# A gated delta rule layer: 8x8 diagonal blocks by substitution on GpSimd instead of three doubling levels, a new order of pieces, and a reordered first stage

## What is computed

```python
h = rmsnorm(x, rms1_w)
q = short_conv(h @ Wq, conv_q_w).reshape(b, t, H, DK)      # 4 taps, then silu; k and v likewise
q, k = (l2norm(q), l2norm(k))
g = -jnp.exp(A_log) * jax.nn.softplus(h @ Wa + dt_bias)
beta = jax.nn.sigmoid(h @ Wb)
def step(S, inp):                                          # scanned over the 256 tokens
    qt, kt, vt, gt, bt = inp
    S = S * jnp.exp(gt)[..., None, None]
    mem = jnp.einsum('bhk,bhkv->bhv', kt, S)
    delta = (vt - mem) * bt[..., None]
    S = S + jnp.einsum('bhk,bhv->bhkv', kt, delta)
    return S, jnp.einsum('bhk,bhkv->bhv', qt * scale, S)
o = rmsnorm(o, gnorm_w) * jax.nn.silu(h @ Wg)
out = x + o.reshape(b, t, VD) @ Wo                         # then the layer's feed-forward part
```

## Time and profile before

| | |
|---|---|
| median of 3 runs | 2594.49 us |
| the profiled execution, its own time | 2592.89 us |
| its span, from the first to the last instruction | 2590.9 us |
| PE busy | 2481.9 us (96%) |
| PE weight loads | 2064.9 us (80%) |
| DVE busy | 2049.2 us (79%) |
| ACT busy | 1700.1 us (66%) |
| POOL busy | 905.7 us (35%) |

### The profile page before, as it was taken

The page is one execution under the profiler, slowest core; times in us unless marked ns, Lnnn a source line. Parts: engine busy times, 40 slices in busy tenths (PEclk is TensorE's granted clock), DMA queues, the critical chain, the costliest instruction groups (busy, mean ns, idle before and its releaser), DMA issues. The chain is left out here.

```text
span 2590.9 us, 59545 instructions
## 1 busy us (share of the span) xinstructions
PE 2481.9 (96%) x22000; PEld 2064.9 (80%) x22000; DVE 2049.2 (79%) x4279; ACT 1700.1 (66%) x3907; POOL 905.7 (35%) x1065
## 2 busy tenths in 40 slices
...
DMA packets 147551, 118.36 MB, mean 46 GB/s; under 512 B 24306, under 2 KB 128699, under 8 KB 147267
## 3 DMA queue, kind: packets, MB, share of 16 engines
...
## 5 line engine op out<-in xcount | busy, mean ns | idle before, releaser
L808 DVE TENSOR_TENSOR dr_w<-dr_ps,mask 128x512 bf16<-128x512 f32 x768 | 526.2, 685 | 88.3 <-PE dr_ps L624 87.8
L822 DVE SCALAR_TENSOR_TENSOR dr_y<-dr_ps,cw,dr_y 128x255 f32<-128x255 f32 (+2 forms) x1152 | 475.7, 473 | 27.1 <-ACT dr_y L938 27.1
L924 ACT CAST dr_tn<-dr_ps 128x512 bf16<-128x512 f32 x640 | 375.2, 586 | 156.0 <-PE dr_ps L637 155.3
L927 ACT CAST dr_tt<-dr_ps 128x512 bf16<-128x512 f32 x768 | 458.7, 597 | 20.7 <-PE dr_ps L644 20.7
L721 PE MATMUL dr_ps<-dr_w,dr_am 128*128 128x96 f32 x3072 | 417.7, 279 | 9.7 <-ACT dr_w L984 2.1
L721 PEld LDWEIGHTS dr_ps<-dr_w,dr_am 128*128 128x128 f32 x3072 | 378.4, 192 | 32.4 <-ACT dr_w L984 24.7
L938 ACT ACTIVATE dr_y<-dr_ps,cw 128x256 f32<-128x256 f32 x384 | 161.3, 471 | 209.9 <-PE dr_ps L661 209.7
L644 PE MATMUL dr_ps<-dr_tt,dr_w 128*128 128x128 bf16 x3072 | 297.3, 219 | 0.9 <-DVE dr_w L808 0.9
L624 PE MATMUL dr_ps<-dr_tn,dr_b 128*128 128x128 bf16 x3072 | 297.1, 219 | 0.0
L1050 POOL TENSOR_SCALAR_AFFINE_SELECT dr_b<-dr_b 128x512 bf16<-128x512 bf16 x128 | 81.9, 640 | 503.7 <-ACT dr_b L974 503.7
L637 PEld LDWEIGHTS dr_ps<-dr_w,dr_tt 128*128 128x128 bf16 x2560 | 186.5, 101 | 84.1 <-issue 49.0
...
## 6 DMA issues: line engine op xcount, KB each, us to landing
...
dr_qk<-dr_sy SPq DMA_DIRECT2D x384, 48.0 KB, 2.0
...
dr_bcb<-scr_b SPq DMA_DIRECT2D x128, 64.0 KB, 4.8
dr_qk<-dr_sy SPq DMA_DIRECT2D x128, 32.0 KB, 1.9
...
```

The costliest lines, as they stand in the source:

```text
L808: v.tensor_tensor((tn if l == 0 else w16)[:, us, :], ps[:, (X0, X1)[g], :].rearrange("p (u n) -> p u n", u=QH), bc(mask[:, l, :], 1, QH), ...
L822: v.scalar_tensor_tensor(y[:, slot, x:T], ps[:, BANK[n], off:off + T - x], cw[:, t, TAPS - 1 - x:TAPS - x], y[:, slot, x:T], ALU.mult, ALU ...
L924: act.copy(tn[:, us, :], ps[:, (X2, X1)[g], :].rearrange("p (u n) -> p u n", u=QH)).then_inc(s["tn_ok"], 1)
L927: act.copy(dst, ps[:, (X0, X2)[g], :].rearrange("p (u n) -> p u n", u=QH)).then_inc(s["tt_ok"], 1)
```

## The change

- `LEVELS` is 4, starting with blocks of size 8 (`LVL0` = 3). The 8x8 diagonal blocks are inverted first: 8 DMAs (`blocks`) copy the diagonal blocks out of `b16` into `c16`; piece `rows` spreads their rows over the partitions with 14 matmuls of 64 columns against selection matrices `sel`, and ACT copies the result to `ab`; piece `base` on GpSimd does the substitution, a copy and 14 small tensor operations, each behind a wait for the one before; piece `expand` on DVE places the 8x8 inverses into 128x128 matrices `tn` and `tt` (a product with a mask, a 32x32 transpose, two products of 128x1024 elements).
- GpSimd's part of `gains` is cut: the root and the scaled keys become pieces `root` and `keys_gain` with places of their own.
- `PLAN` is new; its last piece stands at 56.42, the levels lie between 30.2 and 37.79, the gates come last among an iteration's first pieces, in two PSUM banks.
- `hb` is gone: the projections and gates read `hT`. The gates' weights are loaded on a semaphore of their own.
- In `prepare`: the gate signs are computed on GpSimd, which also makes `sel`; `spread` is issued ahead of `steps`; `scr_b` is written from ACT's queue; the reciprocal and the transposes of `beta` move into `delta_rule`'s first iteration.

```diff
+BASE = 8
-LEVELS = 7
+LEVELS = 4
+LVL0 = 3
-PLAN = ((0.44, ("proj", 0)), (1.01, ("taps", 0, 0)), (2.07, ("proj", 1)), (2.47, ("taps", 0, 1)),
...
+PLAN = ((0.56, ("proj", 0)), (1.72, ("taps", 0, 0)), (2.25, ("taps", 0, 1)), (2.98, ("proj", 1)),
+        (3.59, ("silu", 0)), (3.92, ("taps", 1, 0)), (4.27, ("proj", 2)), (4.33, ("taps", 1, 1)),
+        (4.97, ("taps", 2, 0)), (6.86, ("silu", 1)), (7.7, ("taps", 2, 1)), (7.98, ("gains",)), (8.07, ("norms",)),
+        (8.18, ("keys",)), (8.73, ("silu", 2)), (9.39, ("decays", 0)), (9.46, ("scores", 0)),
+        (9.96, ("decayed", 0, 0)), (10.89, ("decayed", 0, 1)), (11.01, ("decays", 1)), (11.38, ("scores", 1)),
+        (11.92, ("decayed", 1, 0)), (12.74, ("negate", 0)), (12.95, ("decayed", 1, 1)), (13.84, ("negate", 1)),
+        (14.35, ("gate", 0)), (14.42, ("gate", 1)), (15.57, ("root",)), (15.61, ("keys_scale",)),
+        (17.44, ("keys_gain",)), (19.4, ("values", 0)), (21.73, ("values", 1)), (23.28, ("rows",)),
+        (26.88, ("base",)), (29.49, ("expand",)), (30.2, ("merge1", 0, 0)), (30.59, ("merge2", 0, 0)),
+        (30.85, ("merge1", 0, 1)), (32.0, ("merge2", 0, 1)), (32.2, ("merge1", 1, 0)), (33.32, ("merge2", 1, 0)),
+        (33.82, ("merge1", 1, 1)), (34.02, ("merge2", 1, 1)), (34.12, ("merge1", 2, 0)), (34.66, ("merge2", 2, 0)),
+        (34.95, ("merge1", 2, 1)), (35.48, ("merge2", 2, 1)), (36.24, ("merge1", 3, 0)), (36.95, ("merge2", 3, 0)),
+        (37.4, ("round", 0)), (37.53, ("merge1", 3, 1)), (37.79, ("merge2", 3, 1)), (37.94, ("w0", 0)),
+        (38.12, ("residual", 0, 0)), (38.32, ("delta", 0, 0)), (40.47, ("residual", 0, 1)), (40.93, ("delta", 0, 1)),
+        (42.47, ("state_out",)), (43.86, ("mean", 0)), (44.21, ("ks",)), (45.14, ("w0", 1)), (45.23, ("gated", 0)),
+        (46.47, ("residual", 1, 0)), (46.7, ("oT", 0)), (47.83, ("delta", 1, 0)), (48.99, ("residual", 1, 1)),
+        (50.22, ("wo", 0)), (51.24, ("acc", 0)), (51.7, ("delta", 1, 1)), (52.6, ("out", 1)), (52.8, ("mean", 1)),
+        (53.93, ("gated", 1)), (55.19, ("oT", 1)), (55.82, ("wo", 1)), (56.42, ("acc", 1)))
...
             def batch(q, b):
...
-                sp.dma_start(hb[:, m], mem["hT"][:, :, bass.ts(b, T)]).then_inc(s["h_ld"], 16)
...
+            def blocks(it):
+                m = it % NB
+                sp.wait_ge(s["b16_ok"], (it + 1) * CH)
+                wait(sp, s["bc_ps"], it)
+                for n in range(P // (2 * BASE)):
+                    rows = slice(2 * BASE * n, 2 * BASE * (n + 1))
+                    sp.dma_start(c16[rows], b16[rows, m, :, rows]).then_inc(s["c_st"], 16)
...
             for it in range(STEPS):
                 heads_apart(it)
                 if (it + 1) % B == 0 and it + 1 < STEPS:
                     weights((it + 1) // B)
                 if it + 2 < STEPS:
                     batch((it + 2) // B, (it + 2) % B)
+                if (it + 1) % B == 0 and it + 1 < STEPS:
+                    gate_weights((it + 1) // B)
+                blocks(it)
...
+            def rows_(st):
+                it, m = st
+                pe.wait_ge(s["c_st"], (it + 1) * 16 * (P // (2 * BASE)))
+                wait(pe, s["tt_ok"], it * LEVELS * 2 - 1)
+                for j in range(BASE - 1):
+                    for h in range(2):
+                        last = pe.matmul(ps[:, X0, j * U * BASE:(j + 1) * U * BASE], sel[:, h, j, :],
+                                         c16[:, :, h * BASE:(h + 1) * BASE], start=(h == 0), stop=(h == 1))
+                last.then_inc(s["bc_ps"], 1)
...
+            def expand(st):
+                it, m = st
+                v.wait_ge(s["xb_ok"], it + 1)
+                v.tensor_tensor(c32[:].rearrange("p u (r i) -> p u r i", r=4), bc(xb[:], 2, 4),
+                                bc(bc(const[:, C_QUART:C_QUART + 4], 1, U), 3, BASE), ALU.mult).then_inc(s["c32_ok"], 1)
+                v.wait_ge(s["c32_ok"], it + 1)
+                v.transpose(c32t[:].rearrange("p u i -> p (u i)"), c32[:].rearrange("p u i -> p (u i)")
+                            ).then_inc(s["c32t_ok"], 1)
+                wait(v, s["p3"], it * LEVELS * 2)
+                blk = bc(bd32[:].rearrange("p (n i) -> p n i", i=4 * BASE), 1, U)
+                v.wait_ge(s["c32t_ok"], it + 1)
+                v.tensor_tensor(tn[:].rearrange("p u (n i) -> p u n i", i=4 * BASE), bc(c32t[:], 2, 4), blk,
+                                ALU.mult).then_inc(s["te_ok"], 1)
+                v.tensor_tensor(tt[:].rearrange("p u (n i) -> p u n i", i=4 * BASE), bc(c32[:], 2, 4), blk,
+                                ALU.mult).then_inc(s["te_ok"], 1)
...
+            def base(st):
+                it, m = st
+                n = it * (2 * BASE - 2)
+                wait(pool, s["c32_ok"], it)
+                pool.tensor_copy(xb[:], bc(const[:, C_UNIT:C_UNIT + BASE], 1, U)).then_inc(s["xs"], 1)
+                pool.wait_ge(s["ab_ok"], it + 1)
+                for j in range(BASE - 1):
+                    left = BASE - 1 - j
+                    pool.wait_ge(s["xs"], n + 2 * j + 1)
+                    pool.tensor_tensor(xt[:, :, 0:left], bc(xb[:, :, j], 2, left), ab[:, j, :, j + 1:BASE],
+                                       ALU.mult).then_inc(s["xs"], 1)
+                    pool.wait_ge(s["xs"], n + 2 * j + 2)
+                    ins = pool.tensor_tensor(xb[:, :, j + 1:BASE], xb[:, :, j + 1:BASE], xt[:, :, 0:left], ALU.add)
+                    ins.then_inc(s["xb_ok"] if j == BASE - 2 else s["xs"], 1)
```

More of the change, by code:

```diff
@@ L525, in delta_rule @@
         block = ctx.enter_context(nc.Block())
-        SLOTS = 15
-        DEPTH = 4
-        TURN = sorted((x % SLOTS, int(x // SLOTS), piece) for x, piece in PLAN)
         def steps(turn):
@@ L539, in steps @@
                 turn([(i - k, (i - k) % NB) if 0 <= i - k < STEPS else None for k in range(DEPTH)])
+        SLOTS = 15
+        TURN = sorted((x % SLOTS, int(x // SLOTS), piece) for x, piece in PLAN)
         def slots(stages, on):
@@ L553, in delta_rule @@
         PIECES = ("merge1", "merge2", "w0", "delta", "residual", "ks", "out", "state_out", "mean", "gated", "oT", "wo",
-                  "acc", "proj", "silu", "taps", "gate", "norms", "gains", "decays", "keys", "keys_scale", "scores", "decayed", "negate",
+                  "acc", "rows", "base", "expand", "proj", "silu", "taps", "gate", "norms", "gains", "root", "keys_gain", "decays", "keys", "keys_scale", "scores", "decayed", "negate",
                   "values", "round")
@@ L660, in proj @@
                         wt = wqk[:, k, t * P:(t + 1) * P] if t < KTL else wv[:, k, (t - KTL) * P:(t - KTL + 1) * P]
-                        last = pe.matmul(ps[:, BANK[n], j * T:(j + 1) * T], wt, hb[:, m, k, :], start=(k == 0),
+                        last = pe.matmul(ps[:, BANK[n], j * T:(j + 1) * T], wt, hT[:, k, (it % B) * T:(it % B + 1) * T], start=(k == 0),
                                          stop=(k == KT - 1))
                 last.then_inc(s["pj_ps"], 1)
+                if it == 0 and n == 0:
+                    pe.wait_ge(s["bq_ok"], 1)
+                    for j in range(GT):
+                        last = pe.transpose(ps[:, CO, j * P:(j + 1) * P], beta[:, j * P:(j + 1) * P], ident)
+                    last.then_inc(s["bt_ps"], 1)
             def norms(st):
@@ L789, in wo_ @@
                 last.then_inc(s["wo_ps"], 1)
-            on.update(merge1=merge1, merge2=merge2, proj=proj, norms=norms, gate=gate, keys=keys, scores=scores,
+            on.update(merge1=merge1, merge2=merge2, rows=rows_, proj=proj, norms=norms, gate=gate, keys=keys, scores=scores,
                       values=values, w0=w0, residual=residual, delta=delta, out=outputs, state_out=state_out, ks=ks,
@@ L838, in gains @@
                 it, m = st
+                if it == 0:
+                    v.wait_ge(s["bt_ps"], 1)
+                    for j in range(GT):
+                        out = mem["beta"][:].rearrange("p (q g a) (c h) -> p a c g q h", q=NQ, g=GROUPS, c=CH)[:, j // 2, j % 2]
+                        at = ps[:, CO, j * P:(j + 1) * P].rearrange("p (g q h) -> p g q h", g=GROUPS, q=NQ)
+                        v.tensor_copy(out, at).then_inc(s["bq_ok"], 1)
+                    v.wait_ge(s["bq_ok"], 1 + GT)
                 v.wait_ge(s["n_ps"], it + 1)
                 v.wait_ge(s["tap0"], (it + 1) * NT)
+                wait(v, s["nrm_ok"], it)
+                wait(v, s["vo_ok"], (it - NB + 1) * CH)
                 n4 = ps[:, A1, T:T + 2 * U].rearrange("p (c n h) -> p c n h", c=CH, n=2)
@@ L905, in acc @@
                 v.tensor_tensor(at, at, ps[:, CO, 0:D], ALU.add).then_inc(s["acc_ok"], 1)
-            on.update(merge1=merge1, taps=taps, decays=decays, gains=gains, decayed=decayed, values=values,
+            on.update(merge1=merge1, expand=expand, taps=taps, decays=decays, gains=gains, decayed=decayed, values=values,
                       residual=residual, state_out=state, ks=ks, mean=mean, gated=gated, acc=acc)
```

(2 more changed lines are left out.)

289 lines of the change are left out of this document (147 added, 142 removed), and 7 rows, old and new, of the table PLAN.

## The result

The kernel after takes 2519.05 us (median of 4 runs, 2516.61 to 2522.57), the kernel before beside it 2593.88. The ratio is 0.9708, interval 0.9694 to 0.9722: faster by 75 us, where 154 were forecast. 2519 lies inside the range of 2385 to 2550, but only because that range was stretched to rivals 1 and 2, and neither came about as it was told; the turn, and with it the size of the gain, was wrong. The profiled execution has a span of 2516.3 us.

The account below looks back on a forecast made before the run. PE's work bounds a full turn, DVE not far behind. First stage 78.6 + fill 77 + 61 turns 1885 + drain 69 + experts 327.1 = 2436.7 us of span, forecast 2440 us, range 2385 to 2550.

Parts of the forecast that it names:

- Rival 1: DVE keeps its 4.3 us of idle time in each turn: turn 32.5 us, time 2538 us, chance 0.15.
- Rival 2: Both DVE scans hold GpSimd's `base` in full, 1.2 us each: turn 32.4 us, time 2532 us, chance 0.12.
- `rows`: Term of PE's work: 14 added matmuls with a weight load each, 0.78 us a turn (0.42 to 1.55).
- SP's queue: SP issues 21 DMAs an iteration, 15 us of 30.4; both tight places just fit, charged 0.1 to 0.3 us.
- PE's work: PE's turn: 33.22 us less 3.56 for dropped groups of four, plus 0.78 for `rows`, 30.44 if waits stay.
- a sum for all new waits of PE: Added to PE's 30.44 us in each full turn: 0.5 us (0 to 1.2), giving 30.9.
- one loop: From `out` 1 through `mean` 1, `dg`, `base`, selects, `gated` 0 and back: 29.5 us, just under PE's 30.4.
- a busy share of PE under 96%: Sign in full turns that the forecast is wrong; PE's largest summed wait would then tell which rival.
- Rival 3: Each operation of `base` costs as much as `fo`: loop 40.8 us, time 3044 us, chance 0.08 including similar losses.
- Rival 4: Cheaper case: `rows` at 0.42 us, some earlier PE waits gone, turn 30.0, time 2385 us, chance 0.15.
- Fill: Pipeline filling: levels move from the second turn to the third, 88.2 us down to 77 (70 to 85).
- Drain: Pipeline's end: the last piece stands 6.5 slots later, 57.8 us up to 69 (64 to 74).

Follow-up runs that it names:

- e9: Kernel after with the two products of `expand` done in halves, so the first `merge1` waits only for the first half of `tn`: 2499.3 us, ratio 0.963.
- e1: Kernel after with GpSimd's four selects moved behind its two operations of `mean` 0, nothing left out: 2524.5 us, ratio 0.974.
- e11: e9 with `mean` 0 moved behind `expand`, `gated` 0 behind the second mask and GpSimd's selects behind its part of `mean` 0: 2520.4 us, ratio 0.971.
- e2: Kernel after with `base` stopped after three of its seven substitution steps, so the inverses are not those wanted: 2521.1 us, ratio 0.972.
- e14: e9 with only `base`'s copy of xb moved into GpSimd's idle stretch: 2499.7 us, ratio 0.963.
- e4: Kernel after with the product that makes `tn` in `expand` done twice on DVE: 2578.1 us, ratio 0.993.
- e3: Kernel after with the first product of `base` done four times more on GpSimd: 2590.0 us, ratio 0.998.
- e12: Kernel after with the power of `mean` 1 (`fo` on GpSimd) replaced by a product, so the output is not the one wanted: 2481.0 us, ratio 0.956.
- e7: e1 with the two products of `expand` done in halves: 2565.4 us, ratio 0.989.
- e10: e7 with one wait more, so GpSimd's selects begin only once `expand` of the same turn is done: 2508.4 us, ratio 0.967.
- e13: e9 with the second `dg` waiting for the end of the first scan and `base`'s copy moved into GpSimd's idle stretch: 2494.7 us, ratio 0.961.

## Why the prediction failed, step by step

**Right.** First stage: 15.3 us where 13 were forecast. `rows`: 0.60 us (forecast 0.78, bounds 0.42 to 1.55), though the price came from a misread row: `norms` has 6 matmuls, which the row counts as 12, so 0.222 us each and 0.111 for each record, and the 0.055 that was taken for a load rests on no row; measured were 0.043 for each of the 14. DVE's load: 28.2 us forecast, 1724.06 / 61 = 28.3 measured; `expand` is 3.0 from start to start (1023.12 to 1026.12), forecast 2.9. SP's queue: PE waited for `keys`' DMA for 4.0 us in all 61 turns together. The experts didn't change. PE's work: 29.5 against 29.7 by the forecast's own numbers (its 30.44 held the 0.7 of waits that were in the turn of before).

**The step that failed** is "what is left goes into a sum for all new waits of PE: 0.5 us (0 to 1.2)". With the 0.7 that were there before, the forecast had 1.2 us of waits in a turn; the trace has 2.3. This one term, 1.1 us too small, makes 67 us in 61 turns; PE's work came out 0.2 us cheaper, which leaves 59 of the 80 us. I had followed one loop (through `base`, the selects and `gated` 0: 29.5 us) and taken the difference to PE's 30.4 as slack. What the runs show in its place: a loop from `out` 1 through `fo`, `gs`, `dg` and the first scan, behind which three paths part that come together at PE's first `merge1` and the masks. One goes through `scores` 1 and the gates, one through `expand`, one through the copies of b, the selects and `gated` 0. In the kernel after, `expand` is the longest by 0.3 us. e9 shortened it and gained 0.4 us a turn, until `scores` 1 held. e1 shortened the third and gained nothing, e11 shortened `expand` once more, after e9, and gained nothing by it. e2 and e14 cut at `base`, which had slack. e4 lengthened `expand` and paid nearly in full, e3 paid for what went beyond the slack of `base`. e12 shortened what all share and gained 0.56 us for the 0.8 cut. The paths through `scores` 1 and `expand` aren't in the prediction at all, only the remark that a mask will be late "at the first `merge1`". And the sign that it named for its failure, a busy share of PE under 96%, didn't come: the share is 97%, since the records cover the short waits.

**Rival 2**, both scans holding `base` in full, had the right mechanism and the wrong victim. `base` took 6.7 us (forecast 5.8), with 1.17 for a copy that takes 0.24 apart from the scan, and 1.06 for one sum whose neighbours take 0.27; but e2 and e14 show that `base` wasn't on the longest path. The other direction, GpSimd holding DVE, lies on it: the first scan 1.99 us where it needs 1.22, and the product `tn` 1.04 where one of its size takes 0.68 in e4. How much of the miss this is stays open. e7 and e10 show that such a hold can cost 57 us in all, but in another order of the selects; e13, which freed the first scan, gained 0.1 us a turn; e9's 0.4 us come from releasing `merge1` after the first half, with the halves still held (0.59 against 0.42). No run freed both engines of each other and changed nothing else. The Trainium skill (SBUF — State Buffer, Who interferes with whom) says that whichever of the two engines issues first has the port for its whole instruction and the other blocks. The traces agree: the hold goes both ways (select 0.64 to 1.08, half product 0.42 to 0.89), and in the rows around `expand` above each end follows the other engine's: `tn` ends 0.55 us after the select beside it (1024.61, 1025.16), the next select 0.49 after `tn` (1025.65), `tt` 0.54 after that (1026.19), though each had started earlier.

**Rival 1**, DVE keeping 4.3 us of idle time (turn 32.5): it keeps 3.6, and the turn lies between the forecast and this rival. I read the idle time as a consequence of the tied paths; no run tests that by itself. **Rival 3** is out: an operation of `base` costs 0.22 to 0.31 us undisturbed. **Rival 4** too: `rows` takes 0.60 us, not 0.42, and the waits grew.

**Fill, 88.8 and not 77.** Of its three turns (29.7, 27.0, 32.1; before 23.8, 29.7, 34.7) the later two became shorter by 5.3 together, half of the 11 us that the forecast took off the fill. The first grew by 5.9. The plan moved the gates from the middle to the end. In the first turn of the kernel before they stand where PE has nothing else, while `keys` waits for its DMA (timeline of before):

```profile
104.56 2.91 PE L682 MATMUL dr_ps<-wg,dr_hb 128*128 128x384 f32 x4
...
108.05 1.56 PE L682 MATMUL dr_ps<-wg,dr_hb 128*128 128x384 f32 x4 [0.58 <-ACT dr_gs L964]
109.44 0.38 PE L691 MATMUL dr_ps<-const,dr_qk 128*128 128x128 f32 x2
```

and in the kernel after behind all else, at a mean granted clock of 0.63 in that turn:

```profile
93.54 0.69 PE L714 MATMUL dr_ps<-const,dr_qk 128*128 128x128 f32 x2 [3.37 <-DMA dr_qk<-dr_sy]
...
101.42 4.71 PE L705 MATMUL dr_ps<-wg,hT 128*128 128x384 f32 x8 [0.94 <-DVE dr_am L905]
```

From start to start that is 4.6 of the 5.9 us. The rest isn't DVE's reciprocal of beta, which moved from the first stage into this turn (76.13 to 79.48): the first `scores` stand 18.5 us behind the first projection, 18.9 before. It lies around the two pairs of `scores`, which take 2.08 us each where they took 1.14. This is read from the traces, no run undid it. The forecast counted which pieces leave the first turn, not which lose their cover.

**Drain, 78.35 and not 69.** The forecast took the shift of the last piece alone. The levels now lie in the third of the four turns that an iteration takes, so two drain turns hold them and not one; with little beside them they are a chain of product, mask and copy. PE is busy for 20.1 of the first 28.4 us and 22.5 of the next 30.1. Also read, not tried.
